# Turning the scaled B and C tiles by batch on ScalarE in the mixer of a decoder layer

## What is computed

```
proj  = x @ W_in.T                          # gate, value_raw, params
value = silu(causal_conv(value_raw))        # 512 channels = 32 heads x 16
bc    = (value @ W_bc.T).reshape(B, T, 32 heads, 4, 32 states)
bc    = bc / (norm(bc, over states) + eps)  # Bz, Bx, Cz, Cx
def step((z, s), t):                        # for every head, 32 states x 16 channels
    S = 1 / (1 + dt*k + dt*dt*A)
    z = S * (z - dt*A*s + dt*Bz_t*u_t)
    s = s + dt*z + dt*Bx_t*u_t
    y_t = Cz_t . z + Cx_t . s
out = ((y + skip*value) * silu(gate)) @ W_out.T
```

## Time and profile before

| what | value |
|---|---|
| median of 3 runs | 3303.73 us (3301.38 to 3319.04) |
| the profiled execution: time | 3292.49 us |
| the profiled execution: span of its trace | 3290.7 us |
| PE, PEld busy over the span | 2919.8 us (89%), 2169.8 us (66%) |
| DVE, ACT, POOL busy over the span | 2064.4 us (63%), 1304.7 us (40%), 286.7 us (9%) |
| the mixer's 16 units | about 365 to 2095 us of the span |

### The profile page before, as it was taken

The page is one execution under the profiler, slowest core; times in us unless marked ns, Lnnn a source line. Parts: engine busy times, 40 slices in busy tenths (PEclk is TensorE's granted clock), DMA queues, the critical chain, the costliest instruction groups (busy, mean ns, idle before and its releaser), DMA issues. The chain is left out here.

```text
span 3290.7 us, 83944 instructions
## 1 busy us (share of the span) xinstructions
PE 2919.8 (89%) x34208; PEld 2169.8 (66%) x34208; DVE 2064.4 (63%) x7109; ACT 1304.7 (40%) x2250; POOL 286.7 (9%) x227
## 2 busy tenths in 40 slices
PE   5885799999999999999999999589888399999996
PEld 2343577777777877787788777433345166888885
DVE  5444898889889998999899888465562000111110
ACT  3443445454545554545454544133241021333332
POOL 0000000000000000000000000000004700443433
PEclk9887899999999999999999999689899599999998
DMA  6556333542444334433543352200053201778877
GB/s 235 151 151 177 91 85 77 121 104 76 95 117 104 81 95 118 108 83 88 124 104 87 82 128 69 79 1 1 1 203 113 98 28 36 208 201 204 207 200 216
DMA packets 333343, 373.98 MB, mean 114 GB/s; under 512 B 62395, under 2 KB 294988, under 8 KB 328268
## 3 DMA queue, kind: packets, MB, share of 16 engines
q1 hardware_dynamic: 310540, 340.22, 37.6%
q0 software_dynamic: 22464, 28.95, 4.3%
HBM read 269.18 MB, written 104.04 MB: 113 GB/s over the span
## 5 line engine op out<-in xcount | busy, mean ns | idle before, releaser
L604 PE MATMUL ring<-valt,wbc 128*128 128x256 f32 x4096 | 946.2, 387 | 29.0 <-DMA valt<-valt_scratch 26.9
L604 PEld LDWEIGHTS ring<-valt,wbc 128*128 128x128 f32 x4096 | 775.0, 193 | 169.4 <-issue 62.9
L757 ACT COPY bc<-ring 128x512 f32<-128x512 f32 x256 | 149.3, 583 | 739.1 <-PE ring L604 739.1
L917 DVE TENSOR_TENSOR uu<-phi,coef 128x64 f32<-128x64 f32 x2048 | 361.6, 218 | 2.1
L923 DVE TENSOR_TENSOR phi<-phi,uu 128x64 f32<-128x64 f32 x2048 | 361.3, 217 | 0.0
L2039 DVE TENSOR_SCALAR f_yr<-fp_y,f_meta 128x256 f32<-128x256 f32 x124 | 54.3, 480 | 413.3 <-PE fp_y L1856 413.3
L662 PE MATMUL yp<-bc,hpad 32*32 32x64 f32 x8192 | 260.2, 289 | 2.5 <-DVE hc L1023 2.5
L662 PEld LDWEIGHTS yp<-bc,hpad 32*32 32x32 f32 x8192 | 225.3, 121 | 53.3 <-issue 53.0
L1923 ACT ACTIVATE f_hT<-fp_h,f_b 128x256 f32<-128x256 f32 x248 | 117.4, 473 | 327.5 <-PE fp_h L1847 327.5
L1856 PE MATMUL fp_y<-f_w,f_hT 128*128 128x256 f32 x992 | 230.7, 386 | 7.9
L1723 POOL DMA_INDIRECT acc_scratch<-f_yr,f_meta x124 | 192.5, 1553 | 446.7 <-DVE f_yr L2039 300.1
(11 more groups left out here) (227 smaller groups left out, 4070.9 us busy)
## 6 DMA issues: line engine op xcount, KB each, us to landing
f_w<-in_W_dram SPq DMA_DIRECT2D x128, 512.0 KB
coef<-par_scratch SPq DMA_DIRECT2D x128, 256.0 KB, 5.9
fb<-fac_scratch SPq DMA_DIRECT2D x512, 64.0 KB, 2.2
fc<-fac_scratch SPq DMA_DIRECT2D x512, 64.0 KB, 2.8
xg_scratch<-f_fill SPq DMA_DIRECT2D x16, 1032.0 KB, 17.3
f_xr<-xg_scratch SPq DMA_DIRECT2D x64, 258.0 KB
vtok_scratch<-p_vtok SPq DMA_DIRECT2D x32, 512.0 KB, 7.0
dub<-vtok_scratch SPq DMA_DIRECT2D x16, 1024.0 KB, 5.4
```

The lines of the kernel that those rows point to most:

```text
L604: mm = pe.matmul(ring[:, p % 2, v * UT:(v + 1) * UT], wbc[:, k, g, first + v, :], valt[:, u % 2, k, :], start=(k == 0), stop=(k == 3))
L757: nc.scalar.copy(bc[:, gp, first:first + 2, i // 2, :], o).then_inc(bc_ready, 1)
L917: made[k] = mark(V.tensor_tensor(uu[:, k].rearrange("p i (g b) -> p i g b", b=B), phi[:, t, ::-1, k, :].rearrange("p i (g b) -> p i g b", ...
```

## The change

The combined B and C tiles are no longer written back into `bc` by DVE. `inputs` now writes them to a new tile `min` and `read_out` to a new tile `mout` (each 2 x 2 x 256 columns, in place of `m1` and `m2`), in "t b" order as before. ACT then copies them into `bc` in "b t" order (`turn_in`, `turn_out`: two copies each of 128 x 512, reading with a step of 4 elements and writing runs of 64), so that all operands of L629, L642 and L662 have a step of one element. Two semaphores are added, `turned_in` and `turned_out`: PE waits for them in place of `in_ready` and `out_ready`, and DVE waits for them before it writes `min` or `mout` again. There is one `min` and one `mout` for all groups. `post` takes `min` for its scratch, and `uu` and `pend` become views of `min`, so `post`, the first step of `evolve` and `ends` wait for `turned_in` too. `sel` is stored once, as a sliding window, and `resetm` is half as wide: `accumulate` does 16 scans of 128 columns in place of 8 of 256.

```diff
-        sel = sb("sel", [P, G, H])
+        sel = sb("sel", [P, SW])
-        resetm = sb("resetm", [P, UT])
+        resetm = sb("resetm", [P, 2 * L])
-        m1 = sb("m1", [P, 2, UT])
-        m2 = sb("m2", [P, 2, UT])
+        min_ = sb("min", [P, 2, 2, UT])
+        mout = sb("mout", [P, 2, 2, UT])
...
+        def by_batch(gp, c):
+            return bc[:, gp, c].rearrange("p i t -> p (i t)")
...
+        uu = min_[:, 1, 1, 0:4 * LANES].rearrange("p (k i l) -> p k i l", k=2, i=2)
+        pend = min_[:, 1, 1, 4 * LANES:6 * LANES].rearrange("p (i l) -> p i l", i=2)
...
# TensorE, inputs_turned
-                pe.wait_ge(in_ready, n + 1)
+                pe.wait_ge(turned_in, n + 1)
...
-                                          turns(bc[:, gp, v].rearrange("p i t -> p (i t)"))[:, :, b], ident[:])
+                                          by_batch(gp, v)[:, b * P:(b + 1) * P], ident[:])
# TensorE, causal_products (mixed_states in the same way)
-                pe.wait_ge(out_ready, n + 1)
+                pe.wait_ge(turned_out, n + 1)
...
-                                               turns(bc[r, gp, v, i, :])[:, :, b],
-                                               turns(bc[r, gp, 2 + v, i, :])[:, :, b],
+                                               by_batch(gp, v)[r, b * P + i * L:b * P + (i + 1) * L],
+                                               by_batch(gp, 2 + v)[r, b * P + i * L:b * P + (i + 1) * L],
# ScalarE
+            def turn_batches(m, c, gp, done):
+                for v in range(2):
+                    ins = nc.scalar.copy(by_batch(gp, c + v).rearrange("p (b i t) -> p i b t", b=B, i=2),
+                                         m[:, v].rearrange("p i (t b) -> p i b t", b=B))
+                ins.then_inc(done, 1)
+
+            def turn_in(u, gp):
+                act.wait_ge(in_ready, GP * u + gp + 1)
+                turn_batches(min_, 0, gp, turned_in)
+
+            def turn_out(u, gp):
+                act.wait_ge(out_ready, GP * u + gp + 1)
+                turn_batches(mout, 2, gp, turned_out)
...
+                    if gp == 0:
+                        turn_in(u, 0)
                     inputs_turned(u, gp)
                     if more:
                         projected(un, gn, 0)
+                    if gp == 1:
+                        turn_in(u, 2)
+                    if more:
                         projected(un, gn, 1)
+                    if gp == 0:
+                        turn_out(u, 0)
+                    if gp == 2:
+                        turn_out(u, 3)
                     states(u, gp)
...
                     if more:
                         projected(un, gn, 2)
+                    if gp == 0:
+                        turn_in(u, 1)
+                    if gp == 1:
+                        turn_out(u, 2)
+                    if more:
                         projected(un, gn, 3)
                         norms(un, gn)
-                    if gp == 0 and u + 1 < NU:
-                        coefs(u + 1)
+                    if gp == 0:
+                        turn_out(u, 1)
+                        if u + 1 < NU:
+                            coefs(u + 1)
+                    if gp == 1:
+                        turn_in(u, 3)
# VectorE, evolve
                         dve.wait_ge(out_ready, GP * u)
+                        dve.wait_ge(turned_in, GP * u)
# VectorE, accumulate
-                for h in range(2):
+                for h in range(4):
# VectorE, ends
+                dve.wait_ge(turned_in, GP * u + 1)
# VectorE, inputs
+                if n > 0:
+                    dve.wait_ge(turned_in, n)
# VectorE, read_out
-                dve.wait_ge(in_ready, n + 1)
+                if n > 0:
+                    dve.wait_ge(turned_out, n)
# VectorE, post
-                dve.wait_ge(out_ready, read)
+                dve.wait_ge(turned_in, read)
```

42 lines of the change are left out of this document (21 added, 21 removed).

## The result

| | before | changed |
|---|---|---|
| median | 3311.39 us (3301.38 to 3324.01, 4 runs) | 3397.61 us (3390.25 to 3413.37, 4 runs) |
| ratio to before | | 1.0278, 95% interval 1.0223 to 1.0333 |
| profiled execution, its span | 3292.49, 3290.7 us | 3390.25, 3388.4 us |
| granted TensorE clock over the span | 0.937 | 0.908 |

The changed kernel is slower, as forecast, but by 97.7 us of span where the sum had 42. At 3397.61 us it lies above the range that ended at 3382.

The account below looks back on a forecast made before the run. DVE's loop, its instructions plus `fb` waits, was taken to bound. 3.85 us a unit over 14 units is 54, plus 2 for the first, less 9 and 5: 42 us over 3303.7, so 3346 us; range 3296 to 3382.

Parts of the forecast that it names:

- The rival of a gain: Whole loop: PE bounds after all, DVE's `fb` waits shrink as PE runs ahead; -66 us, 3238 us; chance 0.09.
- the one in which the `fb` wait covers it all: Waits at `post` and `evolve` cost nothing, 8 us of scans stand against 14 saved; 3298 us, no change; chance 0.13.
- PE's saving: L662, L642 and the transposes L629: contiguous reads save PE 2.9 us a slot, 11.6 a unit, none on the path.
- PE does not get faster: Rival on PE's products: `evolve` costs 1.5 us more and the 14 us are not saved; +77 us, 3380; chance 0.10.
- The scans: `accumulate` on DVE: 8 more scans a unit over the same columns cost 0.55 us, between 0.3 and 0.9.
- The pair of turns: ACT's two stepped copies of 128 x 512 per turn: 1.2 us a pair, between 1.04 and 2.1.
- The rival made of it: Stepped reads cost ACT double, 2.1 us a pair, so `post` costs 0.9 us more a unit; 3359 us; chance 0.18.
- Place 1: DVE's `post(u, 0)` waits for `turn_in(u, 2)`, 7.4 us late, mostly covered by the `fb` wait; 2.0 us a mean unit.
- Place 3: `turn_out(u, 1)` behind slot (u, 0)'s norms, before `read_out(u, 2)` writes `mout`: ends about when needed; 0, up to 1 us.
- Place 2: `evolve(u + 1)` waits for `turn_in(u, 3)`, done after slot (u, 1)'s norms: 1.1 us plus 0.2 for the clock, sum 1.3.
- A unit's other turns end well ahead of their users.: Remaining turns: `turn_in(u, 0)` runs at once when DVE signals, with `read_out` before DVE asks; no cost in the sum.
- The 14 us taken off: 9.2 us of `km` waits removed by a faster PE, and 5 us at the end where DVE waits for PE.

Follow-up runs that it names:

- pe_only: Kernel before, with TensorE reading `bc` without a step and nobody turning the data (output not the reference's): 0.9961 of the kernel before, unit 110.1 us.
- plain_copies: Changed kernel with ACT's turn copies made without a step, so the tiles are not turned: 1.0224 of the kernel before, unit 115.2 us.
- own_scratch: Changed kernel with the scratch of `post` and `uu` moved out of `min`, their waits for turns gone: 1.0118 of the kernel before, unit 112.1 us.
- turns_early: Changed kernel with `turn_in(u, 2)` moved ahead of the coefficients and `turn_in(u, 3)` ahead of the norms: 1.0116 of the kernel before, unit 113.3 us.
- coefs_late: Changed kernel with ACT's `coefs(u + 1)` moved behind `turn_in(u, 2)` and the next projected piece: 1.0245 of the kernel before, unit 115.8 us.
- turns_out_first: turns_early with `turn_out(u, 1)` also moved ahead of the norms of slot (u, 0): 1.0094 of the kernel before, unit 111.5 us.
- keep_warm_short: Changed kernel with 11 idle TensorE products ahead of the wait for a unit's first turn: 1.0320 of the kernel before, unit 116.5 us.

## Why the prediction was right in direction and short in size

- **DVE's loop bounds, and PE's gain ends in idle time:** held (pe_only, 0.9961). The rival of a gain, that PE bounds after all, falls. So does the one in which the `fb` wait covers it all: it gave up 86.5 us, and the new waits are 190.7.
- **PE's saving.** Taken: 17 and 10 ns for the products of `mixed_states` and `causal_products`. The rows against the earlier trace rows:

```profile
1564.74 1.54 PE L668 MATMUL yp<-bc,hpad 32*32 32x64 f32 x96
...
1580.61 1.59 PE L648 MATMUL kp<-bc 32*64 32x64 f32 x128
```
  96 in about 1.48 us are 15.4 ns, 128 in 1.53 us 12 ns, and the weight load's median is 143 ns. Right within 2 ns; the rival "PE does not get faster" falls. Over the window PE's busy time a unit came down less than the 11.6 us of the prediction, from 106.5 to 98.5 us in pe_only and to 99.4 in the changed kernel, at granted clocks of 0.95 and 0.93 for 0.99.
- **The scans:** 0.4 us a unit for 0.55. Right.
- **The pair of turns:** 2.1 to 2.2 us where I took 1.2. Wrong twice over. I scaled the weight load's penalty, 0.54 ns an element, and let part of it hide behind ACT's pace. Measured against the copies without a step it is 1.0 ns an element, so even the full scaled price, a pair of 1.6 us, was too low. The page that I had set beside it (the Trainium skill, "Advanced Engine Details and Errata", section "Memory Cachelines") was the better guide: by that rule the copies pay, and they do. But this term was not the main failure. The rival made of it gave 3359, and plain_copies shows that price at 0.5 points of 2.8.
- **Place 1, `post`.** Forecast: DVE 7.4 us late there, of which the `fb` wait covers all but 2.0. Measured: 5.63 us of waiting at `post` and 2.04 at `mout` just ahead, 7.7 together, in the unit shown; in the mean 5.5 + 2.1 a unit, and 5.4 us a unit of `fb` wait gone. What is left, 2.2, is the 2.0 of the sum, but the sum had it from `post` alone, and that is in part luck. DVE's factors, whose store and load `fb` waits for, stand behind the wait at `mout`. Before, `fb` came 8.7 us after they began (1498.10 to 1506.78); here they begin at 1573.85, and 8.7 more are 1582.5, while `inputs(u, 3)` starts at 1582.33. So in this unit the 2.04 us at `mout` would have cost as much with no wait at `post`. That agrees with own_scratch and turns_early: they took 136.7 and 87.9 + 34.6 us of waits at `post` and `evolve` away, and `fb` took 73.4 and 77.7 back, which beyond the part of `evolve` leaves 14.5 and 10.2 us for `post`, 0.6 to 0.9 a unit. That ACT's coefficients alone make it was not: coefs_late shows PE's late start just behind them.
- **Place 3, `mout`.** "0, up to 1" was wrong as it stands: 2.0 us in nearly every unit. Beside place 1 it costs little, as place 1 does beside it: in plain_copies the waits at `mout` fell by 18.4 us and those at `post` rose by 14.1. It is left to count once the others are cured (own_scratch, turns_out_first).
- **Place 2, `evolve`.** This is the first step that failed. Forecast 1.3 us, measured 48.8 / 15 = 3.25 a unit. In the unit shown DVE is ready for `evolve` at 1598.67 - 4.14 = 1594.53, and the norms end at 1596.52, 2.0 us behind it, where the sum had them 0.15 ahead; the turn then takes 2.1 us where it had 1.2. The sentence that failed is "that start stays where ACT puts it", on PE's first `summed` of slot (u, 1):

```profile
1569.88 0.22 PE L678 MATMUL yp<-dub,btt 128*32 128x32 f32 x2 [2.93 <-issue]
...
1570.85 1.97 PE L635 MATMUL kp<-ident,bc 128*128 128x128 f32 x8
...
1580.06 0.63 PE L624 MATMUL ssp<-sq,sel 128*32 128x256 f32 x4
```

  DVE is ready for `post` at 1579.90 - 5.63 = 1574.27, so PE's sums come 5.8 us behind that point. Before they came 1504.70 - 1498.44 = 6.3 behind it. But DVE itself reaches it 2.0 us late now, for the wait at `mout`; against DVE's own work PE is 1.6 us later. ACT did not put the start there: PE began the slot only at 1570.85, after standing still for 2.93 us for nothing that the profile shows (DVE's mask for that slot had ended at 1565.8), and at the lower clock, with transposes of 1.97 us. The chain from those sums to the end of the norms took 16.5 us of the 17.2, not the 15.8 forecast: of the 1.4 us taken off, the 0.4 of L662 was never on it, since ACT loads its table for the norms behind the last projected piece.
- **"A unit's other turns end well ahead of their users."** The second step that failed. `turn_in(u, 1)` ends at 1561.99 and DVE wants `min` 1.09 us earlier (L1007): 20.8 us in all, 18.9 of them between the first and the last `ends`, 1.25 a unit, with nothing in the sum for it. ACT does this turn behind the third projected piece, and PE begins that slot after 8.63 us of idle time and at the lower clock. With the clock brought up in keep_warm_short the wait fell from 20.7 to 9.0 us, with cheap copies in plain_copies to 2.0.
- **The 14 us taken off.** The 9.2 at `km` are gone, but hardly by PE's saving, since with that alone (pe_only) they stayed; it is likelier that DVE now comes later. The 5 at the end did not come: the part behind the last `ends` is 0.3 us longer.

By terms, a unit between the first and the last `ends`: 2.2 (places 1 and 3) + 3.25 (place 2) + 1.25 (L1007) + 0.4 (scans) - 0.6 (`km`) = 6.5, where the sum had 3.85 and took the `km` waits off apart. Of the 56 us that the sum was short, place 2 is some 30, L1007 19 and the 5 at the end nearly all the rest. The two steps that failed have one thing in common. Both turns stand in ACT's order behind work that PE must deliver first, and I took PE's starts as they were, while PE now begins its slots later and at the lower clock. That the place behind the norms is what costs at `evolve` is shown (turns_early, 48.8 to 14.2 us). How much of PE's late start of slot (u, 1) comes from DVE's new waits, how much from the pauses and how much from the clock stays open; bringing the clock up ahead of slot (u, 0) left the wait at `evolve` as it was (59.0 and 57.8 us).

## To carry to other kernels

When a copy is handed to an engine that is half idle, its length matters less than its place in that engine's order. Here the tiles lay ready for 13 and 9 us, and moving two copies, or giving two users scratch of their own, took away more than half of the loss. Before a buffer gets a second engine, list every user of it, scratch included, and ask at each when the other engine comes round to it. And a work saving on the engine with the highest share (97% here) is worth only what the other loop leaves: 13 us for 100 here, while one instruction moved on the bounding engine gave as much by the ratio.

## What the runs showed of the hardware

- A step of 16 bytes in fp32 reads costs ScalarE nearly double: 1122 to 1140 ns for 614 on 512 columns. On VectorE, with two stepped operands, 617 for 418 ns on 256 columns and 1085 for 683 on 512; a write with a step of 512 bytes costs the same within 3% (607 and 1062).
- TensorE's small products ran from 30 ns to 15.4 ns each with a contiguous operand. But part of the time comes back as pauses for which the profile shows no releaser. In the kernel before and in pe_only (355 to 2190 us):

```profile
PE yp L682 <- issue: 11.5, 13, 2.6
```

```profile
PE yp L686 <- issue: 28.8, 15, 4.8
```

  That group went from 11.5 to 28.8 us, and the one of `btt` and `dub` ahead of it from 3.9 to 28.4, up to 5.0 us at once. Most fall in the runs of smallest products; what they are was not tried, nor what they cost by themselves.
- After 8.6 us of idle time TensorE began again at a granted clock of 0.50, its first eight transposes took 1.97 us for 1.09, and 11 products of no use in the gap brought those back to 1.09 us, in 11 of 14 units, though not always the 32 products behind them (8.76 us for 7.07). The pause of 2.93 us in the unit above had the same behind it: transposes of 1.97 us again.
